# Self attention of a decoder layer: score tiles of narrow blocks joined in a bank, value products in batches of three and four, joined far maxima

## The chip, the cores and the metric

One Trainium2 chip, one core of it. The time is the device time of one execution in microseconds (us). A core has five engines that run at the same time, each with its own queue, in order: TensorE (matrix products into the PSUM banks), VectorE, ScalarE, GpSimd, and SyncE, which issues transfers (DMAs). They wait for each other on semaphores. TensorE loads its stationary operand by a weight load of its own (PEld in the profile) before each matmul.

## The reference

One encoder and decoder layer: 2 x 2048 target tokens of 512 features, a context of 2 x 77 tokens, 16 heads of 32 features. The target goes through layer norm and causal self attention with a relative bias, cross attention to the encoded context, and a feed-forward part with 2048 hidden features. The part that the change touches is this, with 2048 queries and keys for each head and batch half:

```
scores = q @ k.T / sqrt(32) + rel_bias + causal mask      # bias is one value per distance, constant beyond 127
attn   = softmax(scores)                                   # per query row, with its maximum taken off
out    = attn @ v
```

## The kernel before, in words

Self attention (function `self_attention`, from L1044) goes through 16 steps, one for each of 8 pairs of heads and 2 batch halves. A loop with four steps to the body holds all but the first and last four. In a step the queries lie in four groups g of 512. Scores are computed transposed, 128 keys in the rows and up to 512 queries in the columns, so a group g has 4(g+1) key blocks that causality leaves, 40 in all. One block with both heads is a unit; `SELF_ORDER` (L916) gives their order. A block on the diagonal needs only the queries from its own on, so it is 512, 384, 256 or 128 wide. The function `scores` (L1248) makes two matmuls, one for each head, each into its own one of three PSUM banks (`sa_st`); a bank is free when the exponential of the tile three before it is done. For near blocks VectorE adds the bias in the bank (`bias`, L1355, the instruction in L1363). ScalarE takes the exponential into one of four slots in SBUF (`exponent`, L1292, L1300). `values` (L1258) multiplies it by the values of both heads, in fp32, in two passes for each head, the heads side by side in the array's columns, and adds up over the group in one bank (`sa_ov`); `empty` (L1302) copies that to SBUF, and SyncE stores it.

The maximum of each query row must be known before its scores are made: it goes, negated, into a row of the query operand. So TensorE also makes the scores the other way round, 128 queries in the rows, in chunks of up to 512 keys counted back from the diagonal: a list of 44 maxima steps in a pair (`self_max_steps`, L942), `max_step` (L1230) with two matmuls into one of two double banks (`sa_mp`). VectorE reduces each chunk, head by head (`reduce`, L1325): the chunk at the diagonal (near) by an instruction that adds the distance bias and takes the maximum (L1344, with a read of the accumulator), the others (far) by a plain reduction (L1347). Head h of step a may be issued once head h of step a-2 is reduced. When a group's four query blocks are done, VectorE reduces the chunks' maxima to one per row (L1351), and a turn, one of the 44 steps, transposes it on TensorE (L1239); VectorE negates it (L1330) and SyncE puts it into the query rows with two DMAs (L1141). The first scores of the group wait for that row. The turns of groups 0 to 2 stand two steps into the next group, that of group 3 is last.

The order on TensorE is written out: for each two units the scores of the two units after them, with maxima steps in between by `STEPS_PER_UNIT` (L921, from unit 12 on those of the next pair), and then the value products of the two. VectorE and ScalarE go through the same list for their parts. The first pair's steps 0 to 12 are done in the stage ahead and 13 to 15 at the start; its further steps are packed closer (`OPENING_PER_UNIT`). SyncE loads the next pair's tables and operands at the head of each step (L1118).

Of the kernel before, what the change touches and what calls it, by code (L numbers as in the profile page):

```python
# [28 lines left out]
ALU = mybir.AluOpType  # L29
# [3 lines left out]
P = 128  # L33
# [350 lines left out]
def project(k, io, dr, ident, w, split, pair):  # L384
# [4 lines left out]
    with k:  # L389
# [357 lines left out]
        def _(dve):  # L747
# [130 lines left out]
            for i in range(NG):  # L878
# [4 lines left out]
                for m in range(NM):  # L883
# [32 lines left out]
SELF_ORDER = ((0, 2, 3, 1),  # L916
# [3 lines left out]
STEPS_FROM = 12  # L920
STEPS_PER_UNIT = (2, 2, 1, 0, 2, 0, 1, 0, 2, 1, 1, 1, 2, 0, 2, 1, 1, 0, 2, 1,  # L921
                  1, 2, 1, 1, 2, 1, 2, 0, 1, 1, 1, 2, 1, 0, 1, 1, 1, 2, 0, 1)
INVERSE_AT = 4
OPENING_STEPS = 16
OPENING_PER_UNIT = (3,) * 8 + (2, 2, 0, 0)


def self_units():

    out = []  # L930
    for g, order in enumerate(SELF_ORDER):
        assert sorted(order) == list(range(TT * (g + 1))) and order[0] <= TT * g
        for kb in order:
            i = kb - TT * g
            if i >= 0:
                out.append((g, kb, i * P, min(2 * P, GW - i * P), 0))
            else:
                out.append((g, kb, 0, P if i == -1 else 0, P))
    return out
# [17 lines left out]
def self_steps_at(NU, NM):  # L957

    usual, opening = [[] for _ in range(NU)], [[] for _ in range(NU)]
    a = 0  # L960
    for j, count in enumerate(STEPS_PER_UNIT):
        d, u = (1, STEPS_FROM + j) if STEPS_FROM + j < NU else (0, STEPS_FROM + j - NU)
        usual[u] += [(d, a + i) for i in range(count)]
        a += count
    assert a == NM
    a = OPENING_STEPS
    for u, count in enumerate(OPENING_PER_UNIT):
        opening[u] += [(0, a + i) for i in range(count)]
        a += count
    assert a == NM  # L970
    begun = sum(len(x) for x in usual[STEPS_FROM:])
    u0 = len(OPENING_PER_UNIT)
    for a in range(begun):
        opening[u0 + a * (NU - u0) // begun].append((1, a))
    return usual, opening
# [68 lines left out]
def self_attention(k, name, dr, ident, weights, early, first, pair):  # L1044
# [4 lines left out]
    NU, NM = len(units), len(msteps)  # L1049
    opens = [min(u for u in range(NU) if units[u][0] == g) for g in range(GB)]  # L1050
    ends = {max(u for u in range(NU) if units[u][0] == g): g for g in range(GB)}
    near = [u for u in range(NU) if units[u][3]]
# [5 lines left out]
    usual, opening = self_steps_at(NU, NM)  # L1058
# [3 lines left out]
    ROW = (3 * HD, 3 * HD)  # L1062

    def bank(u, h):
        return (2 * u + h) % NST

    def emptied(u, h):

        j = 2 * u + h
        if j >= NST:  # L1070
            return j - NST
        return max(i for i in range(2 * NU) if i % NST == j) - 2 * NU

    def after(n, u, left):

        for v in (u + 2, u + 3):
            if v < NU:
                yield n, v
            elif left:
                yield n + 1, v - NU  # L1080

    def steps_at(n, u, left):
        steps = opening[u] if isinstance(n.n, int) and n.n == 0 else usual[u]
        return [(n + d if d else n, a) for d, a in steps if left >= d]

    with k:
        qs = [pair.q[0:QK], k.sb(f"{name}_q1", [QK, 2, T], F32R)[:]]
        ks = [pair.k[0:QK], k.sb(f"{name}_k1", [QK, 2, T], F32R)[:]]
        sums = k.sb(f"{name}_sums", [P, H * T // P])
        inv = k.sb(f"{name}_inv", [P, H * T // P])  # L1090
        vs = [pair.v[:, KB * 2 * VW * i:KB * 2 * VW * (i + 1)].rearrange("p (k h e) -> p k h e", k=KB, h=2) for i in range(2)]
        tb = [k.sb(f"{name}_tb{i}", [P, 2, 2 * P]) for i in range(2)]
        ub = [k.sb(f"{name}_ub{i}", [P, 2, GW]) for i in range(2)]
        pr = k.sb(f"{name}_pr", [P, 4, 2, GW])
# [17 lines left out]
        def _(sp):  # L1112
# [34 lines left out]
            for g in range(1, 3):  # L1147
                row(Step(0, 0, UNROLL), g)
# [18 lines left out]
            def slot(n, left):  # L1167
# [5 lines left out]
                if left == 0:  # L1173
                    store_inverses()
# [1084 lines left out]
```

## Time and profile before

| | us |
|---|---|
| median of 3 runs | 2798.24 (2796.01 to 2799.07) |
| span of the profiled execution (the page shows no time around it) | 2800.3 |
| TensorE busy | 2709.4 (97%) |
| VectorE busy | 1583.8 (57%) |
| ScalarE busy | 1261.8 (45%) |

The profiled execution is one run of the kernel. Self attention lies from about 397 to 1609 us of its span, projection and context encoding ahead of it, cross attention from there to about 2070, the feed-forward part last. Ends of matmuls are modelled, and a run of matmuls is shown as one row, from the start of the first to the end of the last, waits inside included.

### The profile page before, as it was taken

The page shows a single profiled execution, that of the slowest core. Times are in us where ns is not written, and L with a number is a line of the kernel's source. Part 1 is how long each engine was busy: PE and PEld are TensorE (multiplying, and loading weights), DVE is VectorE, ACT ScalarE, POOL GpSimd, SP SyncE. Part 2 cuts the span into 40 slices and gives each one's busy share as a digit, 9 for nine tenths or more (in the row PEclk, how much of TensorE's full clock was granted, in tenths as well). Part 3 has the DMA queues.
Part 4 walks back from the last instruction along what each step waited for, and adds up shares of the span by engine and source line. Part 5 has one row for each costly group of instructions (what it writes and reads, how often), then busy time and mean ns, then how long its engine had stood idle before and what let it go on. Part 6 is the DMA issues. An engine that isn't in the chain of part 4 may idle for free. (4 is left out here: it accounts for less than half of the span.)

```text
span 2800.3 us, 40069 instructions
## 1 busy us (share of the span) xinstructions
PE 2709.4 (97%) x12704; PEld 1795.1 (64%) x12704; DVE 1583.8 (57%) x3827; ACT 1261.8 (45%) x2656; POOL 417.8 (15%) x497
## 2 busy tenths in 40 slices
PE   7999989999999999999999899999999999999998
PEld 6788854444444444444444378767778888888886
DVE  5554356777777777777777377567643222122211
ACT  2322113555555555555555545588833322332231
POOL 5000021000000000000000332188556000000000
PEclk9999988999999999999999999999999999999999
DMA  7656653222222222222222398555431000000000
GB/s 223 223 185 209 195 153 83 67 69 69 69 69 69 69 68 58 57 62 61 58 57 68 74 241 262 199 182 181 151 115 47 20 31 31 30 0 30 30 16 15
DMA packets 138949, 272.96 MB, mean 97 GB/s; under 512 B 24885, under 2 KB 56117, under 8 KB 133498
## 3 DMA queue, kind: packets, MB, share of 16 engines
q1 hardware_dynamic: 133530, 255.14, 31.6%
q0 software_dynamic: 5216, 15.33, 1.9%
q8 instruction: 101, 1.65, 0.3%
q14 instruction: 102, 0.84, 0.1%
HBM read 176.02 MB, written 99.98 MB: 99 GB/s over the span
## 5 line engine op out<-in xcount | busy, mean ns | idle before, releaser
L1300 ACT ACTIVATE sa_pr<-sa_st 128x512 f32<-128x512 f32 (+3 forms) x1280 | 611.0, 532 | 542.9 <-DVE sa_st L1363 295.7
L1266 PE MATMUL sa_ov<-sa_pr,sa_v 128*33 128x512 f32 (+3 forms) x2560 | 538.2, 542 | 0.0
L1347 DVE TENSOR_REDUCE sa_part<-sa_mp 128x1 f32<-128x512 f32 x760 | 408.0, 583 | 117.8 <-PE sa_mp L1245 117.0
L1255 PE MATMUL sa_st<-sa_q,sa_k 97*128 97x512 f32 (+3 forms) x1280 | 443.8, 415 | 18.0 <-ACT sa_pr L1300 13.3
L1255 PEld LDWEIGHTS sa_st<-sa_q,sa_k 97*128 97x128 f32 x1280 | 217.8, 191 | 320.2 <-ACT sa_pr L1300 213.3
L1245 PE MATMUL sa_mp<-sa_k,sa_q 96*128 96x512 f32 (+1 forms) x1256 | 364.4, 384 | 9.4 <-PEq L1227 5.3
L1344 DVE CUSTOM_DVE_ANT_0 sa_mp<-sa_mp,sa_ub 128x512 f32<-128x512 f32 (+1 forms) x496 | 308.2, 665 | 80.0 <-PE sa_mp L1245 75.7
L149 PE MATMUL ff_f<-sa_q,ff_w 128*128 128x512 f32 x1024 | 337.2, 391 | 2.9 <-PEq L2066 2.9
L2061 PE MATMUL ff_o<-ff_w,ca_q 128*128 128x512 f32 x1280 | 330.1, 392 | 3.6 <-DVE ca_q L2112 3.6
L2112 DVE TENSOR_TENSOR ca_q<-ca_v,ca_q 128x512 fp32r<-128x512 f32 x128 | 94.9, 741 | 381.1 <-ACT ca_q L2096 381.1
L1266 PEld LDWEIGHTS sa_ov<-sa_pr,sa_v 128*33 128x33 f32 x2560 | 122.5, 111 | 258.4 <-issue 207.6
L1245 PEld LDWEIGHTS sa_mp<-sa_k,sa_q 96*128 96x128 f32 x1256 | 228.1, 194 | 75.7 <-DVE sa_part L1347 22.9
L2061 PEld LDWEIGHTS ff_o<-ff_w,ca_q 128*128 128x128 f32 x1280 | 238.3, 188 | 55.1 <-DVE ca_q L2112 3.7
L2093 ACT ACTIVATE ca_v<-ff_f,ff_b 128x512 f32<-128x512 f32 x128 | 87.7, 686 | 383.7 <-PE ff_f L149 383.7
L1363 DVE TENSOR_TENSOR sa_st<-sa_st,sa_tb 128x256 f32<-128x256 f32 (+1 forms) x608 | 206.1, 380 | 75.8 <-PE sa_st L1255 74.4
L149 PEld LDWEIGHTS ff_f<-sa_q,ff_w 128*128 128x128 f32 x1024 | 193.0, 188 | 43.3 <-PEq L2066 3.3
L149 PE MATMUL ff_f<-sa_k,ff_w 128*128 128x512 f32 x512 | 199.8, 390 | 0.0
L1216 POOL TENSOR_TENSOR sao_ot<-sao_ot,sao_rb 128x512 f32<-128x512 f32 x8 | 10.2, 1273 | 1141.3 <-DMA sao_rb<-scratch_inv 1141.3
L1605 ACT ACTIVATE ca_pq<-ca_s,ca_ng 128x77 f32<-128x77 f32 x512 | 117.6, 342 | 22.4 <-DVE ca_ng L1665 22.1
L149 PEld LDWEIGHTS ff_f<-sa_k,ff_w 128*128 128x128 f32 x512 | 96.6, 189 | 20.2
L149 PE MATMUL qkv_ring<-sa_k,qkv_w 128*128 128x512 f32 x384 | 95.8, 400 | 1.8 <-DVE sa_k L287 1.8
L1507 POOL TENSOR_TENSOR ca_pq<-ca_pq,ca_inv 128x308 f32<-128x308 f32 x128 | 86.7, 698 | 56.5 <-DVE ca_inv L1675 56.4
(240 smaller groups left out, 3283.1 us busy)
## 6 DMA issues: line engine op xcount, KB each, us to landing
sa_q<-scratch_q SPq DMA_DIRECT2D x96, 256.0 KB, 7.6
sa_k<-scratch_k SPq DMA_DIRECT2D x96, 256.0 KB, 8.7
scratch_q<-sao_qst SPq DMA_DIRECT2D x32, 512.0 KB, 6.2
ca_q<-scratch_q SPq DMA_DIRECT2D x32, 512.0 KB, 4.5
scratch_q<-sa_q SPq DMA_DIRECT2D x28, 512.0 KB, 8.0
scratch_k<-sa_q SPq DMA_DIRECT2D x28, 512.0 KB, 5.6
sa_v<-scratch_v SPq DMA_DIRECT2D x16, 528.0 KB, 13.2
scratch_o<-sa_osb SPq DMA_DIRECT2D x128, 66.0 KB
```

Source lines behind the costliest of these rows:

```text
L149: last = pe.matmul(out, s, m, start=(k == 0), stop=(k == n - 1))
L1245: pe.matmul(mp[a % 2][:, h, 0:w], qs[n.par][rows, h, qb * P:(qb + 1) * P], ks[n.par][rows, h, k0:k0 + w], start=True, stop=True).then_inc( ...
L1255: pe.matmul(st[bank(u, h)][:, 0:w], ks[n.par][:, h, kb * P:(kb + 1) * P], qs[n.par][:, h, g * GW + c0:(g + 1) * GW], start=True, stop=True ...
L1266: last = pe.matmul(ov[64 * h:64 * h + VW, c0:GW], vs[n.par][:, kb, h, :], pr[:, u % 4, h, 0:GW - c0], start=(u in opens), stop=(u in ends))
L1300: act.activation(pr[:, u % 4, h, 0:w], st[bank(u, h)][:, 0:w], ACT.Exp, scale=SCALE).then_inc(s["exp"], 1)
L1344: dve.tensor_tensor_reduce(tile, tile, ub[n.par][:, h, GW - w:GW], 1.0, NEG, ALU.add, ALU.max, to)\
L1347: dve.tensor_reduce(to, tile, AX_X, ALU.max).then_inc(s["red"], 1)
L1363: dve.tensor_tensor(tile, tile, tb[n.par][:, h, t0:t0 + w], ALU.add).then_inc(s["bias"], 1)
L1605: last = act.activation(pq_rows[r][:, j, :], sps[n % 3][:, j * S:(j + 1) * S], ACT.Exp, bias=ng[:, r, j:j + 1])
L2061: last = pe.matmul(ops[i][:], a[:, f % 2, t], b[f], start=(f == 0 and n == 0), stop=(f == FC - 1 and n == 2))
L2093: act.activation(hf[:, f % 2, :], fps[f % 2][:], ACT.Relu, bias=b1[:, f:f + 1]).then_inc(s["relu"], 1)
L2112: dve.tensor_tensor(hl[:, f % 2, :], hf[:, f % 2, :], raw(hh[:, f % 2, :]), ALU.subtract)\
```

## The change

In each group the near blocks are re-cut. The block before the diagonal (from group 1 on) and the one on it stay. The fourth (128 wide) and the second (384 wide) share one bank per head, and one bias instruction 384 wide and one exponential 512 wide serve both (`NEAR_PAIR`). The third (256 wide) of both heads share one bank, so one bias and one exponential 512 wide do for both (`NEAR_JOINT`). That gives 36 units with 68 tiles for 40 with 80. The bias table is loaded with its first 128 columns doubled in front (one more DMA). Units are in ten batches of three or four: TensorE now goes, for each batch, through maxima steps and scores of the next batch in turn (step first), then the rest of the steps, then all value products of the batch. Exponentials go to eight slots, two of which, with the sums, are in memory that cross attention uses later. The far chunks of both heads are reduced by one instruction, which waits for both matmuls. The maxima of the next pair begin in batch 5 of 10 (23 of the 44 steps before the pair ends, for 32). SyncE's order of stores and rows is adapted. In the diff, lines taken out are shown only where their place matters; the others stand in the kernel above.

```diff
+BATCHES = ((3,), (4, 3), (4, 4, 3), (4, 4, 4, 3))
+SLOTS = 8
+INVERSE_AT = 1
+NEAR_BEFORE, NEAR_DIAGONAL, NEAR_PAIR, NEAR_JOINT = range(4)
+SELF_ORDER = ((NEAR_DIAGONAL, NEAR_PAIR, NEAR_JOINT),
+              (None, NEAR_DIAGONAL, None, NEAR_PAIR, None, NEAR_JOINT, NEAR_BEFORE),
+              (None, NEAR_DIAGONAL, None, None, NEAR_PAIR, None, None, NEAR_JOINT, None, NEAR_BEFORE, None),
+              (None, NEAR_DIAGONAL, None, None, NEAR_PAIR, None, None, NEAR_JOINT, None, None, NEAR_BEFORE, None,
+               None, None, None))
+STEPS_FROM = 5
+STEPS_PER_BATCH = (4, 5, 4, 7, 3, 2, 6, 3, 4, 6)
+OPENING_PER_BATCH = (7, 7, 6, 6, 5, 4, 4, 4, 4, 4)
+Unit = namedtuple("Unit", "group parts joint biased table")
...
 def self_units():
     out = []
     for g, order in enumerate(SELF_ORDER):
+        d, far = TT * g, iter(range(TT * g - 1))
+        for kind in order:
+            if kind is None:
+                out.append(Unit(g, ((next(far), 0, 0),), False, 0, 0))
+            elif kind == NEAR_BEFORE:
+                out.append(Unit(g, ((d - 1, 0, 0),), False, P, 2 * P))
+            elif kind == NEAR_DIAGONAL:
+                out.append(Unit(g, ((d, 0, 0),), False, 2 * P, P))
+            elif kind == NEAR_PAIR:
+                out.append(Unit(g, ((d + 3, 3 * P, 0), (d + 1, P, P)), False, 3 * P, 0))
             else:
+                out.append(Unit(g, ((d + 2, 2 * P, 0),), True, 2 * P, P))
+        assert next(far, None) is None and sum(BATCHES[g]) == len(order)
+    return out
...
+def self_steps_at(NJ, NM):
+    usual, opening = [[] for _ in range(NJ)], [[] for _ in range(NJ)]
     a = 0
+    for i, count in enumerate(STEPS_PER_BATCH):
+        d, j = (1, STEPS_FROM + i) if STEPS_FROM + i < NJ else (0, STEPS_FROM + i - NJ)
+        usual[j] += [(d, a + x) for x in range(count)]
         a += count
     assert a == NM
+    begun = sum(STEPS_PER_BATCH[:NJ - STEPS_FROM])
     a = OPENING_STEPS
+    for j, count in enumerate(OPENING_PER_BATCH):
+        for _ in range(count):
+            opening[j].append((0, a) if a < NM else (1, a - NM))
+            a += 1
+    assert a == NM + begun
...
+    def emptied(t):
+        return t - NST if t >= NST else max(i for i in range(NTL) if i % NST == t) - NTL
+    def following(n, j, left):
+        if j + 1 < NJ:
+            return [(n, u) for u in batches[j + 1]]
+        return [(n + 1, u) for u in batches[0]] if left else []
+    def places(n, j, left):
+        ahead = following(n, j, left)
+        steps = opening[j] if isinstance(n.n, int) and n.n == 0 else usual[j]
+        steps = [(n + d if d else n, a) for d, a in steps if left >= d]
+        for i in range(max(len(ahead), len(steps))):
+            yield steps[i:i + 1] if i < len(ahead) else steps[i:], ahead[i:i + 1]
+            if i >= len(ahead):
+                break
...
+        pr = k.sb(f"{name}_pr", [P, SLOTS - 2, 2, GW])
+        pr = [pr[:, i] for i in range(SLOTS - 2)] + [early[5][:, 2 * GW * i:2 * GW * (i + 1)].rearrange("p (h t) -> p h t", h=2)
+                                                     for i in range(2)]
...
                 else:
                     load_sums()
                 store(n, 0)
+                row(n, 2)
                 if left == 0:
                     store_inverses()
+                store(n, 1)
                 row(n, 3)
-                store(n, 1)
                 if left == 0:
                     load_second()
+                store(n, 2)
                 if left >= 1:
                     row(n + 1, 0)
                     row(n + 1, 1)
-                store(n, 2)
-                if left >= 1:
-                    row(n + 1, 2)
                 store(n, 3)
             run(sp, N, slot, UNROLL)
...
             def scores(n, u):
+                g, parts, joint, _, _ = units[u]
                 ...
                 for h in range(2):
+                    t = tiles_of[u][0 if joint else h]
+                    if h == 0 or not joint:
+                        waits(pe, s["exp"], NTL * n + emptied(t) + 2)
+                    for kb, c0, at in parts:
+                        at += HALF * h if joint else 0
+                        last = pe.matmul(st[t % NST][:, at:at + GW - c0], ks[n.par][:, h, kb * P:(kb + 1) * P],
+                                         qs[n.par][:, h, g * GW + c0:(g + 1) * GW], start=True, stop=True)
+                    if h == 1 or not joint:
+                        last.then_inc(s["scores"], 1)
...
             def values(n, u):
+                g, parts, joint, _, _ = units[u]
                 ...
+                pe.wait_ge(s["exp"], NTL * n + tiles_of[u][-1] + 2)
+                for i, (kb, c0, at) in enumerate(parts):
+                    for h in range(2):
+                        moving = pr[(NU * n.i + u) % SLOTS][:, 0 if joint else h, :]
+                        at_h = at + (HALF * h if joint else 0)
+                        last = pe.matmul(ov[64 * h:64 * h + VW, c0:GW], vs[n.par][:, kb, h, :],
+                                         moving[:, at_h:at_h + GW - c0], start=(u in opens and i == 0),
+                                         stop=(u in ends and i == len(parts) - 1))
                 last.then_inc(s["av"], 1)
...
-                    if isinstance(n.n, int) and n.n == 0 and u == 0:
+                for j in range(NJ):
+                    if isinstance(n.n, int) and n.n == 0 and j == 0:
                         pe.wait_ge(s["init"], inits)
-                    ahead = list(after(n, u, left))
-                    for i in range(2):
-                        if ahead:
-                            scores(*ahead[i])
-                        for m, a in steps_at(n, u + i, left):
+                    for steps, ahead in places(n, j, left):
+                        for m, a in steps:
                             max_step(m, a)
-                    values(n, u)
-                    values(n, u + 1)
+                        for m, u in ahead:
+                            scores(m, u)
+                    for u in batches[j]:
+                        values(n, u)
             run(pe, N, slot, UNROLL)
...
-                waits(act, s["av"], NU * n + u - 2)
-                for h in range(2):
-                    if u in near:
-                        act.wait_ge(s["bias"], 2 * NB * n + 2 * near.index(u) + h + 1)
+                waits(act, s["av"], NU * n + u - SLOTS + 2)
+                for h, t in enumerate(tiles_of[u]):
+                    if t in near:
+                        act.wait_ge(s["bias"], NB * n + near.index(t) + 1)
                     else:
-                        act.wait_ge(s["scores"], 2 * NU * n + 2 * u + h + 1)
-                    act.activation(pr[:, u % 4, h, 0:w], st[bank(u, h)][:, 0:w], ACT.Exp, scale=SCALE).then_inc(s["exp"], 1)
+                        act.wait_ge(s["scores"], NTL * n + t + 1)
+                    act.activation(pr[(NU * n.i + u) % SLOTS][:, h, 0:width(u)], st[t % NST][:, 0:width(u)], ACT.Exp,
+                                   scale=SCALE).then_inc(s["exp"], 1)
...
                 if isinstance(n.n, int) and n.n == 0 and a == FIRST_STEPS:
                     landed(dve, n, "ub", 1)
-                for h in range(2):
-                    dve.wait_ge(s["chunk"], 2 * NM * n + 2 * a + h + 1)
-                    if chunk == 0:
+                if chunk == 0:
+                    for h in range(2):
+                        dve.wait_ge(s["chunk"], 2 * NM * n + 2 * a + h + 1)
                         dve.sem_inc(s["held"], 1)
-                    tile, to = mp[a % 2][:, h, 0:w], part[:, h, qb, chunk:chunk + 1]
-                    if chunk == 0:
+                        tile, to = mp[a % 2][:, h, 0:w], part[:, h, qb, chunk:chunk + 1]
                         dve.tensor_tensor_reduce(tile, tile, ub[n.par][:, h, GW - w:GW], 1.0, NEG, ALU.add, ALU.max, to)\
                            .then_inc(s["red"], 1)
-                    else:
-                        dve.tensor_reduce(to, tile, AX_X, ALU.max).then_inc(s["red"], 1)
+                else:
+                    dve.wait_ge(s["chunk"], 2 * NM * n + 2 * a + 2)
+                    dve.tensor_reduce(part[:, :, qb, chunk], mp[a % 2][:, :, 0:w], AX_X, ALU.max).then_inc(s["red"], 2)
                 if a in last_of:
                     g = last_of.index(a)
                     dve.wait_ge(s["red"], 2 * NM * n + 2 * a + 3)
...
             def bias(n, u):
+                _, _, joint, w, t0 = units[u]
                 if u == 0:
+                    landed(dve, n, "tb", 2)
+                if w and joint:
+                    t = tiles_of[u][0]
+                    dve.wait_ge(s["scores"], NTL * n + t + 1)
+                    tile = st[t % NST][:].rearrange("p (h t) -> p h t", h=2)
+                    dve.tensor_tensor(tile, tile, tb[n.par][:, :, t0:t0 + w], ALU.add).then_inc(s["bias"], 1)
+                elif w:
+                    for h, t in enumerate(tiles_of[u]):
+                        dve.wait_ge(s["scores"], NTL * n + t + 1)
+                        tile = st[t % NST][:, 0:w]
...
-                    ahead = list(after(n, u, left))
-                    for i in range(2):
-                        if ahead:
-                            bias(*ahead[i])
-                        for m, a in steps_at(n, u + i, left):
+                for j in range(NJ):
+                    for steps, ahead in places(n, j, left):
+                        for m, a in steps:
                             reduce(m, a)
-                    if left == 0 and u == INVERSE_AT:
+                        for m, u in ahead:
+                            bias(m, u)
+                    if left == 0 and j == INVERSE_AT:
                         dve.wait_ge(s["sums"], 16)
```

## Rows read from the trace of the kernel before

**Rows 1.** Timeline, SyncE's table loads: start, duration, queue, line, transfer

```profile
734.38 0.43 SPq L1118 DMA_DIRECT2D sa_ub<-scratch_sa_U  x1
...
1469.74 0.41 SPq L1118 DMA_DIRECT2D sa_ub<-scratch_sa_U  x1
```

**Rows 2.** Waits, 400 to 1600: waiter, releaser, us in total, times, longest

```profile
ACT sa_pr L1300 <- DVE sa_st L1363: 295.7, 267, 4.9
```

**Rows 3.** Timeline, one iteration of two units (operation x count, idle before)

```profile
808.71 0.73 PE L1255 MATMUL sa_st<-sa_q,sa_k 97*128 97x512 f32 x2
...
809.25 1.08 ACT L1300 ACTIVATE sa_pr<-sa_st 128x512 f32<-128x512 f32 x2 [0.51 <-PE sa_st L1255]
809.28 0.40 PE L1245 MATMUL sa_mp<-sa_k,sa_q 96*128 96x256 f32 x2
...
809.52 0.88 PE L1255 MATMUL sa_st<-sa_q,sa_k 97*128 97x512 f32 x2
809.60 0.76 DVE L1347 TENSOR_REDUCE sa_part<-sa_mp 128x1 f32<-128x256 f32 x2 [0.25 <-PE sa_mp L1245]
809.89 0.19 PEld L1255 LDWEIGHTS sa_st<-sa_q,sa_k 97*128 97x128 f32 x1 [0.31 <-ACT sa_pr L1300]
...
810.24 1.09 PE L1245 MATMUL sa_mp<-sa_k,sa_q 96*128 96x512 f32 x4
810.27 0.75 DVE L1363 TENSOR_TENSOR sa_st<-sa_st,sa_tb 128x256 f32<-128x256 f32 x2
...
810.93 0.69 DVE L1344 CUSTOM_DVE_ANT_0 sa_mp<-sa_mp,sa_ub 128x512 f32<-128x512 f32 x1
...
811.26 1.06 PE L1266 MATMUL sa_ov<-sa_pr,sa_v 128*33 128x128 f32 x8
...
812.19 2.48 DVE L1347 TENSOR_REDUCE sa_part<-sa_mp 128x1 f32<-128x512 f32 x4
```

**Rows 4.** Timeline, value products of two units and what follows

```profile
799.78 1.91 PE L1266 MATMUL sa_ov<-sa_pr,sa_v 128*33 128x512 f32 x8
...
801.63 0.73 PE L1255 MATMUL sa_st<-sa_q,sa_k 97*128 97x512 f32 x2
...
807.29 1.48 PE L1266 MATMUL sa_ov<-sa_pr,sa_v 128*33 128x512 f32 x8
```

**Rows 5.** Groups by shape, 400 to 1600: count, busy us, mean ns, idle before

```profile
L1347 DVE TENSOR_REDUCE sa_part<-sa_mp 128x1 f32<-128x512 f32 x478 | 303.4, 681 | 32.4 <-PE sa_mp L1245 31.6
```

**Rows 6.** Timeline, a row's two DMAs; and the table load's time to landing

```profile
825.85 1.25 SPq L1141 DMA_DIRECT2D sa_q<-sa_neg  x2
...
DMA to landing us min/median/max: 2.7/2.8/3.5
```

**Rows 7.** Timeline, TensorE in the first step, six maxima steps in an iteration

```profile
415.97 1.97 PE L1245 MATMUL sa_mp<-sa_k,sa_q 96*128 96x384 f32 x6
...
421.16 1.09 PE L1245 MATMUL sa_mp<-sa_k,sa_q 96*128 96x512 f32 x2 [0.76 <-DVE sa_part L1347]
422.18 1.35 PE L1266 MATMUL sa_ov<-sa_pr,sa_v 128*33 128x128 f32 x8
```

**Rows 8.** Timeline, TensorE, the last value products of self attention

```profile
1604.08 3.63 PE L1266 MATMUL sa_ov<-sa_pr,sa_v 128*33 128x512 f32 x16
```

**Rows 9.** Timeline of TensorE, and stretches: busy by engine, then PEclk, DMA share, GB/s

```profile
447.66 0.37 PE L1239 MATMUL sa_mp<-ident,sa_rmax 128*8 128x128 f32 x1 [2.86 <-DVE sa_rmax L1351]
...
1025.80 0.43 PE L1255 MATMUL sa_st<-sa_q,sa_k 97*128 97x128 f32 x2 [1.64 <-issue]
...
432.00:485.00 53.00, 48.82 (x178) 21.75 (x175) 32.64 (x95) 20.51 (x43) 3.53 (x6) 0.83 0.37 77
485.00:1600.00 1115.00, 1097.83 (x4877) 513.47 (x4876) 846.41 (x2327) 612.03 (x1278) 22.17 (x22) 1.00 0.27 66
...
448.00:462.00 14.00, 13.89 (x43) 6.21 (x43) 4.04 (x17) 4.99 (x10) 0.00 (x0) 0.56 0.22 53
...
1026.00:1034.00 8.00, 7.70 (x24) 4.05 (x24) 4.66 (x12) 2.40 (x6) 0.00 (x0) 0.57 0.53 145
```

More of the change, by code:

```diff
@@ L21 @@
 import math
+from collections import namedtuple
 from contextlib import ExitStack
@@ L931, in self_units, with self_batches @@
     for g, order in enumerate(SELF_ORDER):
[L932 to L936, printed above, removed]
-            else:
-                out.append((g, kb, 0, P if i == -1 else 0, P))
+        d, far = TT * g, iter(range(TT * g - 1))
[8 more added lines that the diff above has]
+                out.append(Unit(g, ((d + 3, 3 * P, 0), (d + 1, P, P)), False, 3 * P, 0))
+            else:
+                out.append(Unit(g, ((d + 2, 2 * P, 0),), True, 2 * P, P))
+        assert next(far, None) is None and sum(BATCHES[g]) == len(order)
+    return out
+def self_batches():
+    out, u = [], 0
+    for size in itertools.chain(*BATCHES):
+        out.append(range(u, u + size))
+        u += size
     return out
@@ L1048, in self_attention @@
     units, msteps = self_units(), self_max_steps()
[L1049 to L1052, printed above, removed]
+    batches = self_batches()
+    NU, NM, NJ = len(units), len(msteps), len(batches)
+    opens = [min(u for u in range(NU) if units[u].group == g) for g in range(GB)]
+    ends = {max(u for u in range(NU) if units[u].group == g): g for g in range(GB)}
+    tiles_of, NTL = [], 0
+    for unit in units:
+        tiles_of.append(range(NTL, NTL + (1 if unit.joint else 2)))
+        NTL += len(tiles_of[-1])
+    near = [t for u in range(NU) for t in tiles_of[u] if units[u].biased]
     NB = len(near)
@@ L1057, in self_attention @@
     NCH = 1 + max(m[3] for m in msteps if m is not TURN)
-    usual, opening = self_steps_at(NU, NM)
+    usual, opening = self_steps_at(NJ, NM)
     inits = 3
@@ L1062, in self_attention, with width @@
     ROW = (3 * HD, 3 * HD)
[L1064 to L1084, printed above, removed]
+    HALF = GW // 2
+    def emptied(t):
[12 more added lines that the diff above has]
+                break
+    def width(u):
+        return GW if units[u].joint else GW - units[u].parts[-1][1] + units[u].parts[-1][2]
     with k:
@@ L1146, in _ @@
             sp.sem_inc(s["row0"], 32)
-            for g in range(1, 3):
-                row(Step(0, 0, UNROLL), g)
+            row(Step(0, 0, UNROLL), 1)
             def load_sums():
```

75 lines of the change are left out of this document (18 added, 57 removed), and 3 rows, old and new, of the table SELF_ORDER.

## The prediction

> **What bounds the kernel now.** I read the page first. TensorE is busy 2709.4 of 2800.3 us, but in self attention that share is no measure of its load: matmul ends are modelled, and a group of instructions waits inside "busy". The stage's pace comes from SyncE's load of the next pair's tables, once per step (one of 16 pairs of heads and batch halves): ten steps lie between 734.38 and 1469.74, so 73.5 us each [rows 1]. The waits say who holds whom: first ScalarE waits for VectorE's bias, 295.7 us [rows 2], and TensorE's weight loads wait for ScalarE to empty score banks. These are chains between three engines, so I followed one iteration in the timeline [rows 3] and took prices and waiting rules from it.
>
> Prices, TensorE. A pair of 512-wide score matmuls takes 0.46 us (808.71 to 809.28 is 0.57, with 0.11 for the first behind value products), 256 wide 0.24 (809.28 to 809.52). Two 512-wide maxima matmuls also take 0.46. Value products of two 512-wide units take 799.78 to 801.63, 1.85 us; of a 512- and a 256-wide one 807.29 to 808.71, 1.42 [rows 4]. So 256 columns cost 0.43 and a 512-wide unit 0.853 (0.64, 0.43, 0.21 for narrower ones), and 0.14 of the 1.85 is the exit. With 0.10 on entering (811.26 lies 1.02 behind 810.24, four matmuls of 0.23 make 0.92) and the 0.11, one change from scores to values and back costs 0.35 us.
> Prices, VectorE. Four 512-wide reductions end after 2.48 us, one lasts 0.68 [rows 3, 5], so each takes (2.48-0.68)/3 = 0.60; 256 wide 0.335 (809.60 to 810.27). That is 1.04 ns an element and 0.07 per instruction. A joined far maximum of 2 x 512 is then 1.13 us for 1.20, and releases its bank 0.08 later. A near maximum (multiply-add form, two heads) takes 810.93 to 812.19, 1.26 us. Bias adds: 256 wide 0.33, 128 wide 0.20, and by the slope 384 wide 0.46, 512 wide 0.60. ScalarE: 0.60 alone, and 1.08 for two, so 0.48 each when it has work.
> Rules. A consumer starts 0.43 us after a 512-wide matmul's start; a blocked weight load starts 0.05 behind its releaser, and the next matmul 0.34 behind that.
>
> A check of these rules on that iteration: scores 0, maxima 0.57, near scores 0.81; the second of these has the bank of the tile whose exponential starts at 0.54 and ends at 1.14, so its weight load is at 1.19 (trace: 809.89, 1.18) and the maxima at 1.53 (810.24, 1.53); values 2.55 (811.26). They meet the trace within 0.02 us.
>
> **The change, part by part.**
> *Value products by fours.* 20 alternations become 10: 10 x 0.35 = 3.5 us off each step. The Trainium skill, TensorEngine Tiling, section Key Properties, says that a change of tiling mode drains TensorE; rows 3 and 4 show such a price as 0.35 us. By that rule alone the sum would be a gain of 16 x 3.5 = 56 us.
> *Narrow blocks sharing banks.* 80 exponentials become 68: less ScalarE work, about 2 us a step, on an engine that waits. The matmuls and their columns stay. Bias goes from 24 x 0.33 + 14 x 0.20 = 10.7 to 9.9 us.
> *Joined far maxima.* 24 x 0.07 = 1.6 us off VectorE, and both heads are waited for and released together. If the engine paid per row of the two-row pattern, it would be 0; at most it is as computed.
> *Sum of work.* Per step TensorE has 17,408 value columns (24 far units of 512, four groups of 1280), 29.0 us; as many score columns for each of two heads, 56 x 0.23 and by the slope 8 x (0.17 + 0.12 + 0.11), 16.1; maxima alike, 15.9; four turns, some 0.8; with 10 changes at 0.35 together 65.3 us (68.8 before, of the measured 73.5, so 5 us of stalls now). VectorE needs 50.6 (52.8 before).
> *Eight slots, moved memory, one more table DMA a step*: nothing; SyncE has gaps, and the slots only let ScalarE be a batch ahead, which the three score banks forbid anyway.
>
> *What the longer value blocks do.* This decides. While four units of values run (up to 3.41 us), TensorE issues nothing else. The maxima have two buffers, so VectorE has then at most two steps (2.3 us) and some biases, and afterwards stands idle until 0.54 us into the next phase. With two units (1.7 us) it hardly ran dry. In the new order TensorE goes (maximum, scores) x 3 or 4, further maxima, then values; VectorE takes each reduction before the bias behind it. I replayed the ten phases with the rules above, each from its first score or maximum to the next. Phase 0 in full: near maximum 0, on VectorE 0.54 to 1.79; far scores 0.57; far maximum 1.03, on VectorE 1.79 to 2.92; the diagonal's scores 1.50 and 1.76, but their bias only at 2.92 and 3.25, exponentials to 3.97 and 4.45. The next unit's second tile needs the first of these banks: 4.13. The pair's two tiles need 4.45 and 4.93 and go at 4.61 and 5.09. Values from 5.46 for 2.13: phase 7.7 for 5.3 of work.
> Phase 4: five reductions and a turn. VectorE 0.66 to 1.53, to 2.79, bias to 3.18, then to 4.31; an exponential behind that bias holds a score bank until 3.72, TensorE goes on at 4.10; reductions to 5.89 and 7.02, the row maximum to 7.33. The turn comes directly behind the last maximum in TensorE's queue, with no values between: TensorE stands from 5.2 to 7.4. Values 7.7 to 10.8, for 7.1 of work.
> All phases, work of TensorE / of VectorE / predicted length: 0: 5.3/4.0/7.7. 1: 7.1/6.4/9.7 (its sixth and seventh reductions hold the maxima buffers until 5.9). 2: 5.7/4.2/7.7. 3: 7.1/5.7/8.0. 4: 7.1/6.3/10.8. 5: 5.9/4.4/7.3 (with 0.3 for row 3: the negation ends at 8.0 of phase 4, two DMAs of 0.62 issue and the second lands some 2.8 later, like the tables [rows 6], at 0.6 of phase 5, where the first scores want it at 0.25). 6: 7.0/5.2/8.9. 7: 6.9/5.1/8.4. 8: 7.6/5.9/9.0 (seven steps: maxima wait for VectorE until 5.2). 9: 5.4/5.5/6.6. Sum 84.1 us a step, against 73.5: +10.6.
> The nearest row that shows such a phase is the opening, where six maxima steps stand in one iteration: from 415.97 to 422.18 there is no value product, and two maxima wait for VectorE [rows 7]: 6.2 us, like the 6.2 that I have in phase 1.
>
> Over the stage: 14 usual steps x 10.6 = 148. The last step has no maxima from phase 5 on and waits for ScalarE there: phases 0 to 4 as above (43.9) and 29.7 for the rest make 73.6, against 64.5 now (from 1469.74 + 73.5 to the end of the last values at 1607.7 [rows 8]), +9. The first step holds 51 maxima steps for 60 now, but in coarser phases; I take 0, between -10 and +10. Sum +157.
>
> *The clock.* In the opening the last turn stands, as it will in each phase 4, right behind its reductions: TensorE idle 2.86 us until 447.66, and from 448 to 462 the granted clock is 0.56 of full, about half of it (1.2 of 2.4 GHz) for most. At 1025.80 an idle of 1.64 us is followed by 0.57 over 8 us; in the rest of 485 to 1600 it is 1.00 [rows 9]. Phase 4 has an idle of 2.2 us in every step. An 8 us stretch at half clock costs at most 3.4 us, where TensorE streams, and values do. I take 2.5 for each of 14 steps, 35 us, with bounds 0 and 14 x 6 = 84 (the 14 us stretch).
> The Trainium skill, TensorE: Matmul & The Clock Gate, section "A second HAM failure mode: psum-queue depth-cycling", tells of a kernel whose short idles between groups of matmuls, with PSUM banks in rotation, made the clock go up and down. Rows 9 agree for two idles. By it, phases 0, 1, 2 and 6, with idles of 1.3 to 1.5 us, would be caught too; that is the slow rival below.
>
> **Forecast.** 2800.3 + 157 + 35 = 2992 by the profiled execution's span, beside which the page shows nothing; this is 2.1 above the median of the runs, so 2990.
>
> **Rivals.**
> *The alternation gain stands and the stalls stay as they are* (faster). For it: TensorE is the engine with most work, and the 5 us of stalls are chains of latency that might shrink with fewer restarts. Then 16 x 3.5 = 56 off, 2742; with no stall at all 16 x 8.2 = 131 off, 2667. Against: VectorE's two buffers, which need no guess. It decides if VectorE is done with a phase's reductions before TensorE is done with its scores. 0.12.
> *Both cancel*, 3.5 us of stalls more a step: 2798. For it: a handful of restarts of 0.5 us would do; against: the replay has three times that. 0.04.
> *The clock oscillates in most phases* (slower still). The stretch of 432 to 485 with its gaps had 0.83 [rows 9]. At that clock the 65.3 us take 13 more; half of it lies in waits: 14 x 6.7 = 94 on top of 157, and up to 182: 3050 to 3140. 0.12.
> *The joined reduction runs slower than its slope*, say as much as two apart plus 0.1: 24 x 0.17 x 14 = 57 more, inside the range. It is within the forecast's case, 0.72.
>
> **Range and chances.** The forecast's own range is 2900 (each phase 0.3 shorter takes 14 x 3 = 42 off, no clock loss 35, and the rest for errors that chain) to 3060. Eight in ten: 2860 to 3080; left out are the fast cases (0.16) and a little of the slowest. A measurement of this kernel tells about 0.2% (5.6 us) from no change. Faster 0.12, same 0.04, slower 0.84.
>
> **What would show it.** SyncE's table loads 84 to 88 us apart instead of 73.5. TensorE waiting for VectorE's row maximum in every step, some 2 us, and low clock behind it. TensorE's waits for ScalarE and VectorE in sum 15 us or more of each step; VectorE busy less than 50 us of each step's 84, at a lower share than now. The joined reduction at 1.2 us. Value groups 10 per step. I am wrong if the steps are below 73.5 us: then VectorE's reductions did not hold the phases, and the place would be phases 0, 1 and 4.

## The result and the profile after

The changed kernel takes 3144.8 us (median of 4, 3136.7 to 3147.2), the kernel before 2797.1: ratio 1.124, 95% interval 1.122 to 1.125. The forecast was slower, 2990, range 2860 to 3080. The direction is right and the size is short by 155 us. The profiled execution has a span of 3134.7 us, 334 over that of before. One of the four executions of scores_first (3959 us) and one of the kernel before in each of two rounds of runs (9026 and 9082 us) were in a slow state of the chip and count in no figure here.

SyncE's table loads of the changed kernel (start, duration, queue, line), which answer to [rows 1]:

```profile
603.89 0.41 SPq L1154 DMA_DIRECT2D sa_ub<-scratch_sa_U  x1
...
989.81 0.43 SPq L1154 DMA_DIRECT2D sa_ub<-scratch_sa_U  x1
...
1380.00 0.43 SPq L1154 DMA_DIRECT2D sa_ub<-scratch_sa_U  x1
```

Eight steps in 776.1 us are 97.0 each, for 73.5 before. The step shown next, one of the shorter ones, takes 95.7 (987.94 to 1083.59). This is TensorE's timeline in it, at the places where it waits (the bracket is the idle time before the row and its releaser), and it answers to [rows 3, 4, 7]. A phase is the stretch from the first score or maximum behind a batch's value products to the next such place; this step's phases 0 and 1 begin at 987.94 and 997.37.

```profile
987.94 0.73 PE L1280 MATMUL sa_mp<-sa_k,sa_q 96*128 96x512 f32 x2
...
992.15 1.88 PE L1293 MATMUL sa_st<-sa_q,sa_k 97*128 97x512 f32 x5 [1.57 <-ACT sa_pr L1342]
993.96 3.48 PE L1309 MATMUL sa_ov<-sa_pr,sa_v 128*33 128x512 f32 x16
997.37 0.73 PE L1280 MATMUL sa_mp<-sa_k,sa_q 96*128 96x512 f32 x2
...
1001.28 0.27 PE L1274 MATMUL sa_mp<-ident,sa_rmax 128*8 128x128 f32 x1 [0.59 <-DVE sa_part L1386]
1002.81 1.30 PE L1280 MATMUL sa_mp<-sa_k,sa_q 96*128 96x512 f32 x4 [1.26 <-DVE sa_part L1390]
...
1010.88 0.72 PE L1293 MATMUL sa_st<-sa_q,sa_k 97*128 97x512 f32 x2 [1.33 <-DMA sa_q<-sa_neg]
...
1030.12 0.50 PE L1293 MATMUL sa_st<-sa_q,sa_k 97*128 97x512 f32 x1 [1.13 <-ACT sa_pr L1342]
...
1033.93 0.37 PE L1274 MATMUL sa_mp<-ident,sa_rmax 128*8 128x128 f32 x1 [2.37 <-DVE sa_rmax L1394]
1034.23 3.39 PE L1309 MATMUL sa_ov<-ca_pq,sa_v 128*33 128x128 f32 x12
...
1049.35 0.49 PE L1293 MATMUL sa_st<-sa_q,sa_k 97*128 97x512 f32 x1 [1.47 <-ACT sa_pr L1342]
```

These are the waits of the replay. The turn stands 2.37 us behind its row maximum (2.2 was predicted), a score tile of phase 0 waits 1.57 for a bank, and phase 1 waits 1.26 for reductions. What was not foreseen in size is in the windows of that step (length, busy time of PE, PEld, DVE, ACT and POOL, then PEclk, DMA share, GB/s); four stretches with value products alone:

```profile
993.96:997.37 3.41, 3.41 (x17) 1.17 (x17) 0.57 (x1) 1.20 (x2) 0.00 (x0) 0.66 1.02 221
...
1034.23:1038.84 4.61, 4.61 (x21) 1.46 (x20) 0.28 (x1) 0.00 (x0) 0.00 (x0) 0.67 0.02 4
1062.36:1065.50 3.14, 3.14 (x21) 1.07 (x21) 0.39 (x2) 0.99 (x3) 0.00 (x0) 1.00 0.00 0
...
1080.89:1083.59 2.70, 2.70 (x13) 0.61 (x13) 2.08 (x4) 1.67 (x3) 0.00 (x0) 1.00 0.00 0
```

The second stretch should take 3.1 us by the prediction's prices and takes 4.61 at a mean clock of 0.67; the third and fourth are at 1.00 and take what the prices say. They also show VectorE running dry: it is busy for 0.28 us of the second's 4.61 and 0.39 of the third's 3.14. In the window 600 to 1500, inside the stage, the clock is 0.89, for 1.00 in [rows 9]; TensorE is busy for 755 of 900 us and VectorE for 510 (57%):

```profile
600.00:1500.00 900.00, 755.14 (x2999) 350.13 (x2996) 510.09 (x1127) 353.24 (x666) 0.00 (x0) 0.89 0.23 55
```

### The profile page after: what moved, and what is told of

The parts are those of the page before. It is cut to its first block and busy times, and to the rows that moved or that the text cites. A ratio compares the mean times of both kernels' runs of the same rounds, so it can differ in the third digit from the quotient of the medians.

```text
span 3134.7 us, 39163 instructions
## 1 busy us (share of the span) xinstructions
PE 2828.2 (90%) x12704; PEld 1844.7 (59%) x12704; DVE 1548.8 (49%) x3255; ACT 1228.4 (39%) x2464; POOL 419.5 (13%) x497
## 5 line engine op out<-in xcount | busy, mean ns | idle before, releaser
L1342 ACT ACTIVATE sa_pr<-sa_st 128x512 f32<-128x512 f32 x808 | 429.5, 602 | 671.2 <-PE sa_st L1293 318.5
L1390 DVE TENSOR_REDUCE sa_part<-sa_mp 128x2 f32<-128x1024 f32 x380 | 383.2, 1022 | 212.4 <-PE sa_mp L1280 211.9
L1309 PE MATMUL sa_ov<-sa_pr,sa_v 128*33 128x512 f32 (+3 forms) x1920 | 471.2, 631 | 0.0
L1280 PE MATMUL sa_mp<-sa_k,sa_q 96*128 96x512 f32 (+1 forms) x1256 | 393.1, 400 | 38.2 <-DVE sa_part L1390 25.4
L1293 PEld LDWEIGHTS sa_st<-sa_q,sa_k 97*128 97x128 f32 x1280 | 239.8, 197 | 308.3 <-ACT sa_pr L1342 178.7
L1280 PEld LDWEIGHTS sa_mp<-sa_k,sa_q 96*128 96x128 f32 x1256 | 221.2, 196 | 205.2 <-issue 114.5
L2108 PEld LDWEIGHTS ff_o<-ff_w,ca_q 128*128 128x128 f32 x1280 | 238.2, 188 | 55.1 <-DVE ca_q L2159 3.7
L1342 ACT ACTIVATE ca_pq<-sa_st 128x512 f32<-128x512 f32 x280 | 150.0, 602 | 142.3 <-PE sa_st L1293 81.6
L1309 PE MATMUL sa_ov<-ca_pq,sa_v 128*33 128x512 f32 (+3 forms) x640 | 163.5, 634 | 0.0
L1411 DVE TENSOR_TENSOR sa_st<-sa_st,sa_tb 128x384 f32<-128x384 f32 (+2 forms) x352 | 141.8, 444 | 42.5 <-PE sa_st L1293 42.1
```

The source lines that it names most:

```text
L1280: pe.matmul(mp[a % 2][:, h, 0:w], qs[n.par][rows, h, qb * P:(qb + 1) * P], ks[n.par][rows, h, k0:k0 + w], start=True, stop=True).then_inc( ...
L1293: last = pe.matmul(st[t % NST][:, at:at + GW - c0], ks[n.par][:, h, kb * P:(kb + 1) * P], qs[n.par][:, h, g * GW + c0:(g + 1) * GW], start ...
L1309: last = pe.matmul(ov[64 * h:64 * h + VW, c0:GW], vs[n.par][:, kb, h, :], moving[:, at_h:at_h + GW - c0], start=(u in opens and i == 0), s ...
L1342: act.activation(pr[(NU * n.i + u) % SLOTS][:, h, 0:width(u)], st[t % NST][:, 0:width(u)], ACT.Exp, scale=SCALE).then_inc(s["exp"], 1)
L1390: dve.tensor_reduce(part[:, :, qb, chunk], mp[a % 2][:, :, 0:w], AX_X, ALU.max).then_inc(s["red"], 2)
L1411: dve.tensor_tensor(tile, tile, tb[n.par][:, h, t0:t0 + w], ALU.add).then_inc(s["bias"], 1)
```

## The experiments

Times are medians of four runs (three for scores_first), and the interval is that of the ratio to the kernel before, run on the same chip. The last column is from the third to the sixteenth table load, for 73.6 before.

| run | us | ratio (95%) | step, mean of 13 |
|---|---|---|---|
| the change | 3144.8 | 1.124 (1.122 to 1.125) | 96.9 |
| pairs | 3013.6 | 1.077 (1.075 to 1.079) | 89.6 |
| filled | 3080.6 | 1.102 (1.100 to 1.104) | 92.9 |
| load_later | 3122.7 | 1.117 (1.115 to 1.119) | 95.8 |
| split_far | 3117.2 | 1.115 (1.112 to 1.117) | 95.4 |
| pairs_late | 2855.4 | 1.021 (1.019 to 1.023) | 77.7 |
| turn_apart | 3120.6 | 1.116 (1.114 to 1.118) | 95.4 |
| scores_first | 3113.8 | 1.113 (1.110 to 1.116) | 95.5 |
| before_joined | 2824.8 | 1.010 (1.008 to 1.012) | 75.3 |
| fours_separate | 3126.4 | 1.118 (1.116 to 1.120) | 95.5 |
| fours_best | 3051.7 | 1.092 (1.090 to 1.094) | 90.3 |
| twos_best | 2844.4 | 1.016 (1.015 to 1.018) | 77.1 |
| filled_late | 3014.8 | 1.077 (1.075 to 1.079) | 88.0 |

**Batches of two** (pairs, pairs_late)

```diff
-BATCHES = ((3,), (4, 3), (4, 4, 3), (4, 4, 4, 3))
+BATCHES = ((3,), (2, 2, 3), (2, 2, 2, 2, 3), (2, 2, 2, 2, 2, 2, 3))
-STEPS_FROM = 5
-STEPS_PER_BATCH = (4, 5, 4, 7, 3, 2, 6, 3, 4, 6)
+STEPS_FROM = 8
+STEPS_PER_BATCH = (3, 3, 3, 3, 3, 2, 3, 3, 3, 3, 2, 3, 3, 3, 3, 1)
-OPENING_PER_BATCH = (7, 7, 6, 6, 5, 4, 4, 4, 4, 4)
+OPENING_PER_BATCH = (5, 4, 4, 4, 4, 4, 3) + (3,) * 5 + (2, 2, 2, 2)
```

> The changed kernel, but its 36 units go in 16 batches of two (one of three at each group's end) for ten of three and four; joined banks, eight slots and joined far maxima stay, and the maxima steps are spread anew, one to three in a phase, with the last turn alone. Theory A (VectorE runs dry in the long value blocks, TensorE then waits for it, and these waits also drop the clock): steps return from 95.6 us to 72 to 77, time 2760 to 2860. Rival B (the joined reductions, which release both heads together, hold TensorE): they are all still there, so steps stay above 88 us, over 3020. Rival C (the clock and the waits come with the joined banks): the same, above 88.

131 us faster than the change, but far from what theory A gave. The timeline of pairs has the reason, a wait for row 2 that this order of the batches makes long:

```profile
969.79 1.22 PE L1293 MATMUL sa_st<-sa_q,sa_k 97*128 97x512 f32 x2 [9.06 <-DMA sa_q<-sa_neg]
```

With batches of two kept and the loads put behind row 2:

> The batches of two units (as in pairs) together with the later loads. In pairs a typical step of 89.7 us has one phase of 17.2 us, in which TensorE waits 9.06 us for row 2's DMAs behind the loads and then runs 13.7 us at half clock; without it its steps would be 89.7 - 13 = 76 or so. Theory A (long value blocks and the clock, and the row as a mishap of pairs alone): steps 73 to 78 us, time 2770 to 2850. Rival B (joined reductions or joined banks cost it): steps stay above 84 us, over 2930.

2855.4, just above the upper end of the range given, and 267 us below load_later, the batches of three and four with the same later loads. Joined banks and joined reductions are all in it, so they are not the main loss. Between these two kernels the maxima steps are spread differently too, one to three in a phase for two to seven; no run has short batches with the coarse spread, so the two can't be told apart.

**The loads behind row 2** (load_later)

```diff
-                if left >= 1:
-                    load(n + 1)
-                else:
+                if left == 0:
                     load_sums()
                 store(n, 0)
                 row(n, 2)
+                if left >= 1:
+                    load(n + 1)
```

> The changed kernel with the next pair's loads issued after row 2 instead of before it, and nothing else. In the changed kernel row 2's two small DMAs are issued at 1003.4, while 12 loads of 256 KB are under way, and its scores start only at 1010.9, with 1.3 us of waiting for them. Theory A with this as a side effect: that wait goes, about 1.3 us in each of 14 steps, 15 to 25 us off, and a little more if a stretch of low clock goes with it. If rows are late for another reason (two DMAs of 2.8 us each in turn): no change within 5 us. If later loads are late for the next maxima: slower by over 10 us.

22 us faster, as expected. In the change the row's two DMAs were issued from 1003.36 on and the scores began at 1010.88; the replay had let them land after 2.8 us [rows 6], as if nothing else was under way.

**Filling TensorE's idle time** (filled, filled_late)

```diff
+            def fill(count):
+                ...
+                    for _ in range(count):
+                        pe.matmul(ov[0:VW, :], ub[n.par][0:3 * HD, 0, 0:VW].bitcast(F32R), ks[n.par][0:3 * HD, 0, 0:GW],
+                                  start=closed, stop=closed)
             def max_step(n, a):
+                fill({28: 2, 29: 5, 43: 9}.get(a, 0))
...
             def scores(n, u):
                 ...
+                if u == 10:
+                    fill(5)
                 ...
+                    if h == 1:
+                        fill({5: 5, 12: 4, 15: 2, 20: 4, 23: 2, 26: 6, 32: 4, 1: 4}.get(u, 0))
```

The weights are columns of the bias table that are set to zero, so the products add nothing to the value bank.

> The changed kernel with 52 more matmuls of 512 columns in each step, all with zero weights and added to the value bank, put in TensorE's queue just ahead of the points where the profile shows it waiting (5 in phase 0, 7 in phase 1, 9 in phase 2, 13 in phase 4, and so on), so that it works where it stood idle. They are some 12 us of work a step and leave the result as it is. If the clock falls because TensorE stands idle for 1.2 to 2.4 us (17 us of each step are at half clock): half clock nearly gone, steps from 95.6 to 87 to 91 us, time 3010 to 3070, faster with more work. If the clock falls for another reason: half clock stays at 17 us and steps are 95 to 100 us. If narrow products (33 columns of weights) don't keep the clock up: the same as the second.

64 us faster, with 52 matmuls of 512 columns more in each step. In the mean of the 13 steps of the table, by the clock that the trace records, half clock fell from 20.0 to 7.1 us. What was left in most steps was one place, around a wait for row 2 that had grown from 1.33 us:

```profile
991.45 1.21 PE L1306 MATMUL sa_st<-sa_q,sa_k 97*128 97x512 f32 x2 [3.57 <-DMA sa_q<-sa_neg]
```

> The changed kernel with the filling matmuls of the run filled and the later loads. In filled the one place left with half clock (6.8 us a step) is phase 1's values and a 3.5 us wait for row 2 behind it; the later loads take that wait away. If idle stretches of TensorE are what the clock follows, no half clock is left in the usual steps, and they show the cost of the waits alone: 84.1 by the replay, plus up to 3 for the filling, so 85 to 89 us, time 2975 to 3035. Against the changed kernel that splits its loss of 22 us a step into some 13 of waits and 9 of clock and row. If the clock falls for another reason: half clock at 7 us a step or more, and time 3050 to 3080.

3014.8, 130 us below the change and inside the range expected; half clock is 0.8 us a step in the mean. The usual steps are 87.4 us, here from the first to the second of two table loads:

```profile
960.90 0.44 SPq L1154 DMA_DIRECT2D sa_ub<-scratch_sa_U  x1
...
1048.35 0.43 SPq L1154 DMA_DIRECT2D sa_ub<-scratch_sa_U  x1
```

Its window of the stage, in the columns as above:

```profile
600.00:1500.00 900.00, 867.45 (x3849) 417.57 (x3847) 561.28 (x1241) 388.94 (x736) 0.00 (x0) 0.99 0.24 58
```

So of the 22.2 us that the step shown grew by (95.7 for 73.5), 8.3 are low clock and the row, and 13.9 are waits at full clock and whatever the filling itself delays. By the means of 13 steps it is 8.9 (96.9 for 88.0) and 14.4.

**Joined reductions** (split_far, before_joined)

```diff
-                    dve.wait_ge(s["chunk"], 2 * NM * n + 2 * a + 2)
-                    dve.tensor_reduce(part[:, :, qb, chunk], mp[a % 2][:, :, 0:w], AX_X, ALU.max).then_inc(s["red"], 2)
+                    for h in range(2):
+                        dve.wait_ge(s["chunk"], 2 * NM * n + 2 * a + h + 1)
+                        dve.tensor_reduce(part[:, h, qb, chunk:chunk + 1], mp[a % 2][:, h, 0:w], AX_X, ALU.max)\
+                           .then_inc(s["red"], 1)
```

> The changed kernel with the far maxima reduced head by head again, as before the change: 24 x 0.063 us more work for VectorE in each step, but each head's half bank is free when it is reduced. Theory A: VectorE's chain decides in the phases 1, 4 and 8, so 0.3 to 1 us slower a step, time 3145 to 3160. Rival B (joined reductions hold TensorE): faster by 3 us a step or more, under 3100.

> The kernel before with one part of the change alone: the far maxima of both heads by one instruction. VectorE has 24 x 0.063 = 1.5 us less work a step; but the first head's half bank comes free 0.5 us later, and the reduction starts 0.23 later. Theory A holds that joining is nearly neutral: within 10 us of 2797. Rival B (in the run with split reductions the changed kernel was 27 us faster, so joining costs): 2810 to 2840.

Theory A fails here, and rival B's size (under 3100) was not reached either. Head by head the change is 28 us faster, 1.5 us a step, and joining alone makes the kernel before 27 us slower, 1.7 us a step, although the joined instruction costs what the slope said. In the kernel before this happens at full clock (half clock is under 1 us a step with and without it). In split_far a part of the gain is clock: half clock is 16.3 us a step for 20.0. The timeline of the change:

```profile
1029.54 1.22 DVE L1390 TENSOR_REDUCE sa_part<-sa_mp 128x2 f32<-128x1024 f32 x1
...
1031.20 2.36 DVE L1390 TENSOR_REDUCE sa_part<-sa_mp 128x2 f32<-128x1024 f32 x2 [0.45 <-PE sa_mp L1280]
```

Two in 2.36 us, one lasts 1.22, so 1.14 each for 2 x 0.60. What is left as a cause is the start, which waits for both heads, or the release of both halves of the bank at once. This is argued, and which of the two it is was not tried.

**The last turn apart, and scores ahead** (turn_apart, scores_first)

```diff
-STEPS_PER_BATCH = (4, 5, 4, 7, 3, 2, 6, 3, 4, 6)
+STEPS_PER_BATCH = (4, 5, 4, 7, 3, 3, 6, 4, 5, 3)
```

> The changed kernel with the same order of everything but the number of maxima steps in phases 0 to 4: 3, 6, 4, 5, 3 for 2, 6, 3, 4, 6. The last turn then stands behind two steps with scores between, and no longer right behind three reductions. Theory A with the clock: phase 4 loses the 2.4 us idle, some 3 us of reductions and its stretch of half clock, phases 0, 2 and 3 take one step more each (1 us each where VectorE holds them): 0 to 3 us less a step, time 3100 to 3145. If the clock's falls there don't cost: within 10 us of 3145, or slower.

24 us faster, 1.5 us in the mean step. Phase 4 went from 12.6 to 9.5 us, but it kept its stretch of half clock, now behind a wait of 1.41 us for the turn. Phase 3, which had one step more and had gone at full clock in 8.1, took 11.0 with 3.4 us at half clock: most of the gain went there. The second kernel swaps maxima step and scores in each place, on TensorE and VectorE:

> The changed kernel with scores ahead of the maxima step at each place, on TensorE, and the bias ahead of the reduction on VectorE, as the kernel before had it. Theory A says that part of the loss is the diagonal's bias behind two reductions (phases 0 and 2: 1.5 us of waits for a score bank): 0.5 to 2 us less in phases 0, 2, 6 and 7 each, steps 89 to 93 us, time 3060 to 3110. Rival: the order makes no difference, since VectorE has the same work in a phase: 3130 to 3160. Phase 5 then opens with scores that want row 3, which may give 0.5 us of it back.

31 us faster, just short of the range expected. Phases 0 and 6 got shorter (9.4 to 7.3 and 10.7 to 8.0), but the scores that need row 2 now come first in phase 2 and wait longer for it: from the start of phase 1 to the first of them there are 16.7 us for 13.5.

**The parts together** (fours_separate, fours_best, twos_best). The first has 40 units in batches `((4,), (4, 4), (4, 4, 4), (4, 4, 4, 4))`, each narrow block with its own banks, in an order of its own (`SELF_ORDER`); the other two are the change, in fours and in twos, and all three have the edits of load_later, split_far and scores_first.

> Everything of the change taken back but the batches: 40 units with their own banks again, far maxima head by head, scores ahead of maxima steps, and loads issued after row 2 so that no row waits behind them; value products by fours from eight slots (ten batches of four), with the changed kernel's maxima steps. It stands against the kernel before for the batches alone. Theory A (the batches are the cause): most of the loss is there, steps 84 to 92 us, time 2950 to 3080. Rival (the loss comes from the joins and the row): below 2870.

3126.4: batches of four, without any join, cost nearly as much as the whole change, and more than was expected. Against the kernel before it also differs in the order of the units, the spread of the maxima and the place of the loads, and these were not taken apart. Its clock in the window is 0.90:

```profile
600.00:1500.00 900.00, 776.74 (x3058) 350.51 (x3053) 536.89 (x1481) 374.45 (x795) 0.00 (x0) 0.90 0.23 55
```

> The changed kernel with three parts mended, each of which was faster by 22 to 28 us alone: loads after row 2, far maxima head by head, scores ahead of the maxima. Batches of three and four and joined banks stay. If the three act on different waits they add up, and more, as in scores first the row's wait had grown to some 5 us a step in phase 1's tail: steps 84 to 88 us, time 2960 to 3040. If one wait hides the other: 3060 to 3110. Theory A wants it well above the same kernel in twos.

3051.7, between the two ranges expected: the three mends gave 81 us singly (22, 28 and 31) and 93 together. fours_separate has the same three mends and is 75 us slower. So what else sets the two apart, joined banks with batches of three and another order of the units, gains when the batches are long; how much of it is the banks is open.

> The same three mends in batches of two (one of three at each group's end), with joined banks. From 2855 for the twos with later loads, less some 27 for reductions head by head, less what the order gives in the phases with a diagonal (0.5 to 1 us a step, 10 to 15 us): 2800 to 2830; it has 16 changes between scores and values in a step for 20 before (1.4 us a step less), so 2770 to 2800 is open if the spread of the maxima is as good as the old one. Theory A: 150 us or more below fours_best.

2844.4, below fours_best by 207 us and at full clock, but above the range expected: the two further mends gave 11 us on pairs_late, not the 37 or more that they were put at. fours_best and twos_best differ in the batches and, with them, in the spread of the maxima, and in nothing else. Its first and ninth table load of the stage:

```profile
592.58 0.45 SPq L1154 DMA_DIRECT2D sa_ub<-scratch_sa_U  x1
...
1210.84 0.43 SPq L1154 DMA_DIRECT2D sa_ub<-scratch_sa_U  x1
```

That is eight steps in 618.3 us, 77.3 each. VectorE is busy for 73% of the window, for 57% in the change:

```profile
600.00:1500.00 900.00, 848.46 (x3777) 404.31 (x3773) 656.05 (x1704) 443.61 (x840) 0.00 (x0) 1.00 0.27 64
```

But it is not below the kernel before: 77.1 us a step for 73.6, with four changes between scores and values fewer. Its spread of the maxima, its order of units, its joined banks and its batches of three differ from before; which of them costs the 3.5 us is open. No kernel here beats the one before.

## Why the prediction was short

*Where the loss is, and its sign: right.* The longer batches, with the coarser spread of the maxima that goes with them, are the cause (fours_best 1.092 against twos_best 1.016; fours_separate 1.118). No run isolates the gain of 3.5 us a step from fewer changes; whatever it is, the waits ate more.

*The replay of the waits: right in mechanism, a little low.* Phase by phase, predicted and measured (from the starts of the phases in the trace): 7.7 and 9.4; 9.7 and 11.5; 7.7 and 9.3; 8.0 and 8.1; 10.8 and 12.6; 7.3 and 7.3; 8.9 and 10.7; 8.4 and 8.7; 9.0 and 11.2; 6.6 and 6.9. In phases 3, 5, 7 and 9, which no half clock touches and which wait little for a row, the sum is 31.0 for 30.3. Phase 2 has no half clock either; its excess of 1.6 is mostly the wait for row 2. The term was +10.6 us a step; filled_late has +13.9, with its fillings.

*The step that failed: the clock's term, "I take 2.5 for each of 14 steps, 35 us".* I let only phase 4's idle of 2.2 us bring the clock down. In the trace the step shown has five stretches of half clock (1.2 GHz) of 3.4 us each, 17 us in all: behind idles of 1.57 us in phase 0, 0.59 and 1.26 in phase 1, 1.13 and 2.37 in phase 4, 1.47 in phase 6, and several waits below 0.3 each in phase 8. 13.2 of the 17 us lie in value products, where they cost half, 6.6 us. With 1.3 for row 2 that is 7.9, and filled_late gives 8.3. In the mean of the 13 steps it is 20.0 us of half clock, 15.4 of them in value products, so 7.7 us for the clock and 9.0 with the row, where the means of filled_late give 8.9. So the clock's term, by this working, is 14 x 7.7 = 108 us for my 35, beyond even my bound of 84. That filling TensorE's idle time takes the half clock away (20.0 to 7.1 to 0.8 us a step) shows that idle time brings nearly all of it. The slow rival (0.12, 3050 to 3140) said this: its 6.7 us a step is close to what was measured, and its range ends 5 us below the result. The Trainium skill, TensorE: Matmul & The Clock Gate, section "A second HAM failure mode: psum-queue depth-cycling", tells of a clock that goes up and down with short idles while PSUM banks are in rotation. The trace agrees, with five falls in one step. The sign that it would happen stood in [rows 9]: from 430 to 1600 the kernel before has two idles over 0.9 us, 2.86 and 1.64, half clock came with both, and the replay had five of 1.3 to 2.2 us in a step. Its chance should have been larger than that of the forecast.

*The whole miss.* From the third to the sixteenth table load the change is 303 us longer, in the last two steps 37, and up to the third load 6 us shorter (the opening was taken as 0): 334 by the profiled spans for 192 predicted. By this working, of the 142 that were missing the clock is about 73 (14 x 5.2), row 2 18, and further waits of 3.7 us a step, which the replay did not have, 52; the last step adds 5 and the opening takes 6.

*Row 2: missed.* The replay placed its DMAs 2.8 us before landing [rows 6]; behind twelve loads of 256 KB it took 7.5 us. In pairs and scores_first TensorE's wait for it grew from 1.3 to 9.1 and 4.4 us.

*The last step:* from its table load to the end of the values the last two steps take 175.2 us for 138.0, so the last one is 14 to 15 us longer (by the mean step and by the step shown), for 9.

*Joins: "nothing" for the banks, a small gain for the reductions.* The first stands untested alone. The second was wrong in sign: joining costs 1.5 to 1.7 us a step. The prediction counted only a release 0.08 us later; but the first head's half of the bank, which TensorE can fill by itself, is free some 0.5 us later than head by head.

*VectorE's work.* The prediction has 50.6 us a step in its sum of work, but its ten phases add up to 52.7, and one of its signs was "less than 50". The trace has 55.1 busy us in each of the 13 steps (57.2 before), at a share of 57%: the lower share came true, the figure did not. TensorE's waits, put at 15 us a step or more, are 15.6 in the window, the row's with them.

## What to carry to other kernels

When a change groups work on the busiest engine, replay the other engines' queues through the longer block: a double buffer covers two pieces and no more, and what the partner can't do in the block it does while the first engine waits. Then ask of each wait in the replay whether it lowers TensorE's clock; here the fall cost about half as much as the waits (7.7 us a step beside some 14). Fewer restarts are worth little beside that (0.35 us each by the prediction's prices, an estimate that no run isolates).

## What was not expected of the hardware

52 more matmuls a step, with zero weights, made the kernel 64 us faster (filled), and with the wait for row 2 removed as well the clock was at 0.99 of full, for 0.89. Idles of 1.26, 1.47 and 1.57 us were followed by 3.4 us at half clock, those of 1.33 and 1.17 in phase 2, 1.17 in phase 7 and 1.16 in phase 9 were not, and phase 8 had a fall with no idle over 0.3: the length of one idle does not tell it.
